# A two-layer AdaLN feed-forward kernel on one core: half-wide turns in the opening, two bias rows sent through DRAM, the last down chunk and one query product moved

## The chip, the cores and the metric

The kernel runs on one NeuronCore of a Trainium2 chip. Five engines work side by side, each with its own instruction queue: TensorE (matrix products and turns, PE in the profile), VectorE (DVE), ScalarE (ACT), GpSimd (POOL) and the queue of SyncE (SP), which here only issues DMAs. They meet through semaphores. The metric is the device time of one execution in microseconds; lower is better.

## The reference

The input x is 32 samples of 32 channels by 512. Two layers are added to it one after the other:

```python
# layer 0: grouped conv (9 taps), plus a row per sample and channel
h = conv1d(x, w, groups=4, pad=4) + (cond @ c_weight.T)[:, :, None] + bias
shared = relu(h @ up_w) ** 2 @ down_w
routed = ((h @ fc1) @ expert) * sum_of_top2(h @ gate_w) @ fc2
x = x + layernorm(shared + routed) * gamma + beta
# layer 1: per-sample mixing of channels, att from a small MLP on cond
att = softmax(gelu(gelu(cond @ W0 + b0) @ W1 + b1) @ W2 + b2)
y = einsum(att @ weight, x) + (att @ bias_k)[:, :, None]
q, k = y @ Wq.T, y @ Wk.T                  # 8 experts of 32
s = softmax(sum(q * k) per expert / sqrt(32))
x = x + y @ W.T + b + sum_e s_e * (y @ A_e.T) @ B_e.T
```

All is float32. Large products are made of three products of rounded halves: with a = a_hi + a_lo, a @ b is a_hi b_hi + a_hi b_lo + a_lo b_hi (`mm3`, lines 1215 to 1219).

## The kernel before, in words

The 1024 rows (sample, channel) are 8 tiles of 128, `T` from 0 to 7, in two halves `h` of four tiles. The order of work on each engine is written out by hand, and an engine does its list strictly in that order.

**Opening (lines 1410 to 1449).** TensorE multiplies ones seven times while the first loads land, turns the padded conv weights in 12 transposes of 128x128 (line 1418) and the conditioning rows in one (line 1424), and does the convs of tiles 0 to 3 (`conv`, line 1233). ScalarE and VectorE make the shifted copies of x that the convs read. VectorE forms the 32 context rows (`rows`, line 991: conditioning product plus bias) and folds them by a 0/1 mask into `fold128`, 32 samples wide, of which TensorE's products with ones spread the rows over the partitions: `conv_bias` (line 1246) adds samples 0 to 15 to the conv banks of the first half, and one product at line 1448 makes `B0`, the rows of samples 16 to 31 on all partitions, which ScalarE copies out (line 722). `B0` is used by `add_ctx` (line 873) in the second half. Between them the expert weight is multiplied with fc2 (12 products, lines 1441 to 1446).

**Each half (lines 1495 to 1521).** There are 8 chunks of the hidden dimension. `up(i)` makes chunk i in PSUM bank `U[i % 2]`; ScalarE takes `relu` of it (line 666), VectorE squares it (909), ScalarE rounds it into `R_hi` (672), VectorE writes the rest into `R_lo` (913, semaphore `s_R`). `up(i)` for i of 2 or more waits for `s_R` of chunk i-2, since it takes its bank. `down(i)` adds chunk i into the four banks `D[t]`. The first two chunks are made in parts of 256 columns: `up(0)` and `up(1)` left, `up(0)` right, `gate_rows` (lines 1257, 1258), `up(1)` right, `gate_logits`, `up(2)`, two `latent` products, and then `down` and `up` in turn. ScalarE does relu of chunk 0, `gate_copy`, `up_split` of chunk 0, relu of chunk 1. In the first half VectorE splits the four tiles of `H` (line 884) and up weights (863) in the order H0, up0, H1, up1, H2, H3. The buffer `relu` lies in the memory that the opening's small buffers, `rows` among them, had.

**Between the halves.** At the end of the first half TensorE does `down(6)`, `mixing` (lines 1461, 1466), `down(7)`, `conv(4)`, `mixing_bias` (line 1476: two products with ones that spread the 32 rows att @ bias_k, folded by VectorE with the mask, over the partitions; ScalarE copies them to `B1`), `conv(5)` to `conv(7)`, and the second half's `up(8)`. VectorE does per tile `norm_stats` (three instructions, lines 947 to 956), then, once GpSimd has the reciprocal root, `norm_apply` (line 964, semaphore `s_x1`), and `add_ctx` and `split_H` (873, 889) for tiles 4 to 7. The four parts of `down(8)` wait for `s_x1` of tiles 0 to 3, `up(8)` for the split tiles.

**Tail (lines 1524 to 1553).** Per tile `mix`, `qk` (24 products of 320 columns), `dense` (12 of 512), `turn_hw` and `combine`; `qk(7)` waits for the split weights of tile 5 (`s_hwT`, line 1154), whose bank it takes. `finish` adds into X, and SP stores it.

**The queues of DMA.** SP issues all weight loads at the start in one row: x in four parts, up, fc, down (2 MB), the last 1 MB of x, gamma, beta (`rowb`), then waits for the fc2 split, and issues the conditioning loads, three of the mixing weights and 32 of Wq and Wk. ScalarE issues only the store of the gate sums (`sum_rows`), its spread, and the last output.

Of the kernel before, what the change touches and what calls it, by code (L numbers as in the profile page):

```python
# [16 lines left out]
def bass_adaln_ffn(  # L17
# [84 lines left out]

    sum_rows = nc.dram_tensor("sum_rows", [HALVES, P, TPH], F32, kind="Internal").ap()

    with ExitStack() as ctx:
# [65 lines left out]
        aggb_hl = sb("aggb_hl", [2 * N, C], F32R)  # L171
        attT3 = sb("attT3", [96, N], F32R)
        attT2 = sb("attT2", [KE, 2, N])
        turn2 = sb("turn2", [2 * N, N])
        bk = sb("bk", [KE, C])
        with ExitStack() as early:
            def se(name, shape):
                return sb(name, shape, F32, early)
            cc_nat = se("cc_nat", [P, CD])
# [5 lines left out]
            wc_pad = se("wc_pad", [P, NWIN * PH + PH - 1, C])  # L185
            gmask = se("gmask", [C, G])
            exraw = se("exraw", [P, LC, LAT])
# [37 lines left out]
        fold2 = H_lo[0:2 * N, 0:2].rearrange("k a b -> k (a b)").rearrange("k (n o) -> k n o", o=C)  # L225
        agg = qk_raw[0:C].rearrange("i c a q -> i (c a q)")[:, 0:N * C].rearrange("i (o n) -> i o n", n=N)
        fold128 = up_hi[:, IC - 2:IC].rearrange("k c p q -> k (c p q)").rearrange("k (n o) -> k n o", o=C)
# [31 lines left out]
        s_ccz = sem("s_ccz")  # L259
# [13 lines left out]
        s_rowsb = sem("s_rowsb")  # L273
# [3 lines left out]
        s_B0p = sem("s_B0p")  # L277
# [22 lines left out]
        s_B1p = sem("s_B1p")  # L300
# [153 lines left out]
        def _(sp):  # L454
# [22 lines left out]
            sp.dma_start(rowb[:], L0_ffn_ln_beta.partition_broadcast(P)).then_inc(ld_gb, 16)  # L477
            sp.wait_ge(s_fc2, 1)
# [4 lines left out]
            sp.dma_start(b2, L1_cond_b2.partition_broadcast(N)).then_inc(ld_cond, 16)  # L483
            sp.wait_ge(s_wkz, 1)
# [138 lines left out]
        def _(act):  # L623
# [87 lines left out]
            split_up(1)  # L711
            split_H(2)
            split_H(3)
            act.wait_ge(ld_gate, 16)
# [6 lines left out]
            act.wait_ge(s_B0p, 1)  # L721
            nc.scalar.activation(B0[:], M[1], ACT.Copy).then_inc(s_B0, 1)
# [20 lines left out]
            def copy_attT():  # L743
                act.wait_ge(s_aTp, 1)
                nc.scalar.activation(attT3[:], M[0][0:96, 0:N], ACT.Copy).then_inc(s_aT, 1)
                nc.scalar.activation(attT2[:], bcast_mid(M[0][0:KE, 0:N], 2), ACT.Copy).then_inc(s_aT, 1)

            def make_B1():
                for i in range(2):
                    act.wait_ge(s_B1p, i + 1)  # L750
                    nc.scalar.activation(B1[:, i * BANK:(i + 1) * BANK], M[i], ACT.Copy).then_inc(s_B1, 1)

            for h in range(HALVES):
                i0 = h * IC
                if h:
                    make_B1()
# [94 lines left out]
        def _(dve):  # L851
# [14 lines left out]
            def add_ctx(T):  # L866

                dve.wait_ge(s_conv, T + 1)
                if T == TPH:
                    dve.wait_ge(s_B0, 1)  # L870
# [97 lines left out]
            nc.vector.memset(cc_nat[N + C:P], 0.0).then_inc(s_ccz, 1)  # L968
# [15 lines left out]
            def fold_rows(to, hl):  # L984

                return nc.vector.tensor_tensor(to, bcast_mid(hl[:].bitcast(F32), N),
                                               turn2[:].unsqueeze(2).broadcast_to([2 * N, N, C]), ALU.mult)

# [10 lines left out]
            fold_rows(fold, rows_hl).then_inc(s_rows, 1)  # L999
# [6 lines left out]
            split_up(1)  # L1006
            split_H(2)
            split_H(3)
            dve.wait_ge(s_gateh, 1)
# [37 lines left out]
            def fold_aggb():  # L1047
                dve.wait_ge(s_aggbp, 1)
                nc.vector.tensor_copy(aggb_hl[:], U[0][0:2 * N, 0:C]).then_inc(s_aggb, 1)
                dve.wait_ge(s_aggb, 1)  # L1050
                nc.vector.tensor_tensor(aggb_hl[N:2 * N], U[0][N:2 * N, 0:C], aggb_hl[N:2 * N].bitcast(F32),
                                        ALU.subtract).then_inc(s_aggb, 1)
                dve.wait_ge(s_aggb, 2)
                fold_rows(fold2, aggb_hl).then_inc(s_rowsb, 1)
# [8 lines left out]
            for h in range(HALVES):  # L1063
                i0 = h * IC
                if h:
                    split_attT()
                    fold_aggb()
                    turn_agg()
                    norm_stats(0)
                    norm_stats(1)  # L1070
                    norm_apply(0)
                    norm_stats(2)
                    norm_apply(1)
                    add_ctx(TPH)
                    norm_apply(2)
                    split_H(TPH)
                    for T in range(TPH + 1, TILES):
                        add_ctx(T)
                        split_H(T)
                    norm_stats(3)  # L1080
                    norm_apply(3)
                up_square(i0)
                up_split(i0)
                gate_sum(h)
                up_square(i0 + 1)
                if h == 0:
                    split_E2()
                up_split(i0 + 1)
                if h == 0:
# [24 lines left out]
            def y_bias(T):  # L1114

                dve.wait_ge(s_yp, T + 1)
                b = mix_bank(T)
# [96 lines left out]
        def _(pe):  # L1214
# [6 lines left out]
            def conv(T):  # L1221

                if T == TPH:
                    pe.wait_ge(s_R, IC)
                    pe.wait_ge(s_aggb, 2)
                if T == TPH + 2:
                    pe.wait_ge(s_lat, LC)
                    pe.wait_ge(s_B1, 2)
# [32 lines left out]
            def gate_logits(h):  # L1261

                pe.wait_ge(s_gTs, h + 1)
                if h == 0:
                    pe.wait_ge(s_B0, 1)
                else:
# [6 lines left out]
            def up(i, part=None):  # L1273
# [4 lines left out]
                if part is None:  # L1278
                    part = slice(0, TOKH)
                if c < 2:  # L1280
                    pe.wait_ge(s_H, TPH * h + part.stop // P)
# [4 lines left out]
                for p in range(PH):  # L1286
                    last = mm3(U[i % 2][:, part], up_hi[:, c, p], up_lo[:, c, p], H_hi[:, p, part],
                               H_lo[:, p, part], p == 0, p == PH - 1)
                if part.stop == TOKH:
                    last.then_inc(s_upp, 1)  # L1290
# [73 lines left out]
            def dense(T):  # L1364
# [4 lines left out]
                for p in range(PH):  # L1369
# [53 lines left out]
            pe.wait_ge(s_ccz, 1)  # L1423
            nc.tensor.transpose(M[0][:, 0:P], cc_nat[:], ident[:]).then_inc(s_cTp, 1)
# [16 lines left out]
            for lc in range(LC):  # L1441
                for mc in range(LC):
# [13 lines left out]
            def mixing():  # L1456
# [4 lines left out]
                nc.tensor.matmul(U[0][0:2 * N, 0:C], attT2[:].rearrange("k a n -> k (a n)"), bk[:],  # L1461
# [7 lines left out]

            def mixing_bias():  # L1470

                pe.wait_ge(s_rowsb, 1)
                pe.wait_ge(s_agg, 2)
                flat = fold2.rearrange("k n o -> k (n o)")
                for i in range(2):
                    nc.tensor.matmul(M[i], ones_r[0:2 * N, :], flat[:, i * BANK:(i + 1) * BANK],  # L1476
                                     start=True, stop=True).then_inc(s_B1p, 1)
# [105 lines left out]
```

## Time and profile before

| | us |
|---|---|
| median of 3 runs (219.13 to 219.44) | 219.26 |
| the profiled execution | 220.35 |
| its span, first to last instruction | 218.4 |
| TensorE busy | 214.3 (98%) |
| VectorE busy | 126.8 (58%) |
| ScalarE busy | 81.1 (37%) |
| GpSimd busy | 62.0 (28%) |

```profile
## 2 busy tenths in 40 slices
PE   7999999999999999999999999999999999999995
PEld 7999988888887778998888888888998998999984
DVE  4895455869725579876462034445996537435443
ACT  6694853549484621224322033442013112121110
POOL 3037221340464622119400002443354202202000
PEclk9999999999999999999999999999999999999999
DMA  6999944400000000046534000000000110110103
```

A slice is 5.46 us, and each digit is the busy share of an engine in tenths. TensorE shows 9 throughout. The sixteen DMA engines are full up to the fifth slice, that is to about 27 us, and half busy for three slices more. A busy TensorE is not TensorE at its peak, since matmuls are pipelined; the chain of work that ended last says how much time each group takes.

### The profile page before, as it was taken

How to read it: one execution, taken by the hardware profiler on the slowest of the kernel's cores; microseconds unless marked ns; L12 is line 12 of the kernel's file. 1: busy time of each engine (PE TensorE's matmuls, PEld its weight loads, DVE VectorE, ACT ScalarE, POOL GpSimd, SP SyncE). 2: the span in 40 equal slices, each digit the busy share in tenths (PEclk: the TensorE clock that was granted, in tenths of full speed). 3: DMA queues.
4: the chain of work that ended last, by engine and by line, in shares of the span. 5: the costliest groups of instructions: out<-in, count | busy, mean ns of one | idle time of the engine just before them, and what ended most of it. 6: DMA issues, size and time to landing. Idle time of an engine off the chain costs nothing.

```text
span 218.4 us, 3221 instructions
## 1 busy us (share of the span) xinstructions
PE 214.3 (98%) x1210; PEld 188.6 (86%) x1210; DVE 126.8 (58%) x268; ACT 81.1 (37%) x157; POOL 62.0 (28%) x77
## 2 busy tenths in 40 slices
PE   7999999999999999999999999999999999999995
PEld 7999988888887778998888888888998998999984
DVE  4895455869725579876462034445996537435443
ACT  6694853549484621224322033442013112121110
POOL 3037221340464622119400002443354202202000
PEclk9999999999999999999999999999999999999999
DMA  6999944400000000046534000000000110110103
GB/s 150 328 411 405 271 68 98 63 0 0 3 0 0 0 0 3 0 65 102 104 42 79 3 0 0 0 0 5 0 0 0 48 51 0 50 51 0 48 0 144
DMA packets 31087, 14.14 MB, mean 65 GB/s; under 512 B 25224, under 2 KB 26056, under 8 KB 31072
## 3 DMA queue, kind: packets, MB, share of 16 engines
q1 hardware_dynamic: 30256, 13.26, 22.2%
q10 hardware_dynamic: 816, 0.69, 1.1%
q8 instruction: 9, 0.15, 0.3%
q14 instruction: 6, 0.05, 0.1%
HBM read 11.84 MB, written 2.10 MB: 64 GB/s over the span
## 4 chain that ended last, share of the span: by engine, by line
PE 97%; DVE 1%; issue 0%; ACT 0%; DVEq 0%
PE PS L1217 26%; PE PS L1219 25%; PE PS L1218 25%; PE PS L1233 10%; PE PS L1346 3%; PE PS L1408 2%; PE PS L1418 1%; PE PS L1258 1%; PE PS L1257 1%; PE PS L1246 0%; PE PS L1375 0%; DVE ring L913 0%; PE PS L1476 0%; PE PS L1466 0%; ACT ring L672 0%
## 5 line engine op out<-in xcount | busy, mean ns | idle before, releaser
L909 DVE TENSOR_TENSOR PS<-PS,relu 128x512 f32<-128x512 f32 x16 | 11.2, 699 | 31.9 <-ACT relu L666 31.7
L1217 PE MATMUL PS<-H_hi,up_hi 128*128 128x512 f32 (+1 forms) x80 | 28.3, 354 | 0.2 <-DVE ring L913 0.2
L1219 PE MATMUL PS<-H_hi,up_lo 128*128 128x512 f32 (+1 forms) x80 | 27.8, 347 | 0.0
L1218 PE MATMUL PS<-H_lo,up_hi 128*128 128x512 f32 (+1 forms) x80 | 27.8, 347 | 0.0
L1233 PE MATMUL PS<-wconv,XS 128*128 128x128 f32 x192 | 22.5, 276 | 0.0
L1233 PEld LDWEIGHTS PS<-wconv,XS 128*128 128x128 f32 x192 | 21.9, 192 | 0.6 <-issue 0.4
L1217 PE MATMUL PS<-qkT_hi,H_hi 128*128 128x320 f32 x64 | 19.8, 310 | 0.1
L1219 PE MATMUL PS<-qkT_hi,H_lo 128*128 128x320 f32 x64 | 19.8, 309 | 0.0
L1218 PE MATMUL PS<-qkT_lo,H_hi 128*128 128x320 f32 x64 | 19.8, 309 | 0.0
L588 POOL TENSOR_TENSOR X<-X,rowb 128x512 f32<-128x512 f32 x8 | 10.3, 1297 | 28.1 <-PE PS L1346 28.1
L1217 PE MATMUL PS<-dn_hi,ring 128*128 128x512 f32 x44 | 17.4, 395 | 0.0
L666 ACT ACTIVATE relu<-PS 128x512 f32<-128x512 f32 x16 | 9.5, 593 | 21.2 <-PE PS L1219 19.5
L1219 PE MATMUL PS<-dn_hi,ring 128*128 128x512 f32 x44 | 17.2, 390 | 0.0
L1218 PE MATMUL PS<-dn_lo,ring 128*128 128x512 f32 x44 | 17.1, 389 | 0.0
L1217 PEld LDWEIGHTS PS<-H_hi,up_hi 128*128 128x128 f32 x80 | 15.1, 189 | 2.2 <-issue 0.3
L1219 PEld LDWEIGHTS PS<-H_hi,up_lo 128*128 128x128 f32 x80 | 15.1, 189 | 1.9
L1218 PEld LDWEIGHTS PS<-H_lo,up_hi 128*128 128x128 f32 x80 | 15.2, 189 | 1.9
L560 POOL TENSOR_TENSOR dn_lo<-dn_raw,dn_hi 128x512 fp32r<-128x512 f32 x8 | 10.3, 1290 | 21.7 <-ACT dn_hi L648 21.7
L450 ACT ACTIVATE XS<-X 32x128 f32<-32x128 f32 (+2 forms) x24 | 15.8, 658 | 0.6 <-DMA X<-in_x_dram 0.3
L449 DVE COPY XS<-X 32x128 f32<-32x128 f32 (+2 forms) x40 | 15.2, 380 | 0.6
L592 POOL TENSOR_TENSOR wT_lo<-qk_raw,wT_hi 128x512 fp32r<-128x512 f32 x4 | 5.1, 1291 | 31.9 <-ACT wT_hi L700 31.9
L1217 PE MATMUL PS<-wT_hi,H_hi 128*128 128x512 f32 (+1 forms) x36 | 13.7, 381 | 0.0
(196 smaller groups left out, 477.3 us busy)
## 6 DMA issues: line engine op xcount, KB each, us to landing
up_raw<-in_L_ffn_up_w_dram SPq DMA_DIRECT2D x2, 1024.0 KB, 9.7
dn_raw<-in_L_ffn_down_w_dram SPq DMA_DIRECT2D x2, 1024.0 KB, 13.9
out_dram<-X SPq DMA_DIRECT2D x7, 256.0 KB, 2.0
X<-in_x_dram SPq DMA_DIRECT2D x1, 1024.0 KB, 15.1
XS<-in_L_ffn_W_dram SPq DMA_DIRECT2D x16, 64.0 KB, 2.4
X<-in_x_dram SPq DMA_DIRECT2D x2, 256.0 KB, 3.4
X<-in_x_dram SPq DMA_DIRECT2D x1, 512.0 KB, 5.8
fc<-in_L_ffn_fc_w_dram SPq DMA_DIRECT2D x1, 512.0 KB, 6.4
```

Of the source, the lines that this page charges most:

```text
L449: return nc.vector.tensor_copy(dst, src)
L450: return nc.scalar.activation(dst, src, ACT.Copy)
L560: nc.gpsimd.tensor_tensor(dn_lo[:, c, :], dn_raw[:, c, :], dn_hi[:, c, :].bitcast(F32), ALU.subtract).then_inc(s_dn, 1)
L588: nc.gpsimd.tensor_tensor(X[:, T, :], X[:, T, :], rowb[:], ALU.add).then_inc(s_x1b, 1)
L592: nc.gpsimd.tensor_tensor(wg_dst(g, False), wg_turned(g), wg_dst(g, True).bitcast(F32), ALU.subtract)\
L666: nc.scalar.activation(relu[:], U[i % 2], ACT.Relu).then_inc(s_relu, 1)
L909: nc.vector.tensor_tensor(U[i % 2], U[i % 2], relu[:], ALU.mult).then_inc(s_sq, 1)
L1217: nc.tensor.matmul(o, lh, rh, start=start, stop=False)
L1218: nc.tensor.matmul(o, lh, rl, start=False, stop=False)
L1219: return nc.tensor.matmul(o, ll, rh, start=False, stop=stop)
L1233: last = nc.tensor.matmul(conv_bank(T)[:, s * P:(s + 1) * P], XS[:, T % TPH * SPT + s, a:a + P], wconv[:, a], start=(a == 0 and (T >= TPH ...
L1346: last = nc.tensor.matmul(mix_bank(T)[:, p, :], X[:, T, p * P:(p + 1) * P], BD[:, T], start=True, stop=True)
```

## The change

1. The padded conv weights and the conditioning rows get 64 partitions for 128, and the 13 transposes take a 64x64 identity: 64 columns for 128. The memset on the unused rows goes.
2. The context rows are folded for 16 samples only. `B0` is made by DMA: SP stores 16 rows to DRAM and reads them back spread over the partitions; the product of line 1448 and its copy go. Relu of chunk 0 now also waits for the store, whose source it overwrites.
3. `B1` goes the same way, late: the fold, `mixing_bias` and its copies go.
4. `up(0)`, `up(1)`, `up(8)` and `up(9)` are made in whole columns; the splits of H2 and H3 go ahead of the one of up1.
5. `down(7)` comes after the convs of the second half, and VectorE's norm steps between the ones of the second half.
6. In the tail a quarter of `dense(6)` comes between `combine(4)` and `qk(7)`.

```diff
@@ sync
+            sp.wait_ge(s_ctx, 1)
+            sp.dma_start(ctx_rows, rows[N // 2:N]).then_inc(s_ctxw, 16)
             sp.wait_ge(s_fc2, 1)
...
             sp.dma_start(b2, L1_cond_b2.partition_broadcast(N)).then_inc(ld_cond, 16)
+            sp.wait_ge(s_ctxw, 16)
+            sp.dma_start(B0[:], ctx_rows.rearrange("n o -> (n o)").partition_broadcast(P)).then_inc(s_B0, 16)
             sp.wait_ge(s_wkz, 1)
...
+            sp.wait_ge(s_aggb, 1)
+            sp.dma_start(mix_rows, aggb[:]).then_inc(s_mixw, 16)
+            sp.wait_ge(s_mixw, 16)
+            sp.dma_start(B1[:], mix_rows.rearrange("n o -> (n o)").partition_broadcast(P)).then_inc(s_B1, 16)
             sp.wait_ge(s_xb, TILES)
@@ scalar
             def up_relu(i):
                 act.wait_ge(s_upp, i + 1)
+                if i == 0:
+                    act.wait_ge(s_ctxw, 16)
...
-            split_up(1)
             split_H(2)
             split_H(3)
+            split_up(1)
...
-            act.wait_ge(s_B0p, 1)
-            nc.scalar.activation(B0[:], M[1], ACT.Copy).then_inc(s_B0, 1)
@@ vector
-            fold_rows(fold, rows_hl).then_inc(s_rows, 1)
+            nc.vector.tensor_tensor(fold, bcast_mid(rows_hl[:].bitcast(F32), N // 2),
+                                    turn2[:, 0:N // 2].unsqueeze(2).broadcast_to([2 * N, N // 2, C]), ALU.mult)\
+                .then_inc(s_rows, 1)
...
-            def fold_aggb():
+            def copy_aggb():
                 dve.wait_ge(s_aggbp, 1)
...
+                nc.vector.tensor_copy(aggb[:], U[1][0:N, 0:C]).then_inc(s_aggb, 1)
...
                 if h:
                     split_attT()
-                    fold_aggb()
+                    copy_aggb()
                     turn_agg()
+                    for T in range(TPH, TILES):
+                        add_ctx(T)
+                        split_H(T)
                     norm_stats(0)
                     norm_stats(1)
                     norm_apply(0)
+                up_square(i0)
+                if h:
                     norm_stats(2)
+                up_split(i0)
+                if h:
                     norm_apply(1)
...
+                else:
+                    gate_sum(h)
+                up_square(i0 + 1)
+                if h:
+                    gate_sum(h)
                     norm_stats(3)
...
                 up_split(i0 + 1)
+                if h:
+                    norm_apply(2)
+                    norm_apply(3)
@@ tensor
-                    last = nc.tensor.transpose(M[1][:, o0:o0 + P],
-                                               wc_pad[:, k0:k0 + PH, :].rearrange("p k c -> p (k c)"), ident[:])
+                    last = nc.tensor.transpose(M[1][:, o0:o0 + 2 * C],
+                                               wc_pad[:, k0:k0 + PH, :].rearrange("p k c -> p (k c)"),
+                                               ident[0:2 * C, 0:2 * C])
...
-            nc.tensor.matmul(M[1], ones_r[:], fold128[:, N // 2:N, :].rearrange("k n o -> k (n o)"),
-                             start=True, stop=True).then_inc(s_B0p, 1)
...
                 if h:
                     conv(TPH)
-                    mixing_bias()
                     for t in range(1, TPH):
                         conv(TPH + t)
-
-                for i in (h * IC, h * IC + 1):
-                    up(i, slice(0, TOKH // 2))
-                up(h * IC, slice(TOKH // 2, TOKH))
+                    down(IC - 1)
+
+                up(h * IC)
                 gate_rows(h)
-                up(h * IC + 1, slice(TOKH // 2, TOKH))
+                up(h * IC + 1)
                 gate_logits(h)
                 up(h * IC + 2)
                 for n in range(LC):
                     latent(h * LC + n)
-                for c in range(IC):
+                for c in range(IC if h else IC - 1):
                     down(h * IC + c)
...
             combine(a)
+            dense(c, range(0, 1))
             qk(d)
-            dense(c)
+            dense(c, range(1, PH))
```

## Rows read from the trace of the kernel before

**Rows 1.** part 4 of the page: the chain that ended last, by engine
```profile
PE 97%; DVE 1%; issue 0%; ACT 0%; DVEq 0%
```

**Rows 2.** waits of TensorE: tile, line <- releaser: us in total, times, longest
```profile
PE PS L1217 <- DVE ring L913: 0.2, 1, 0.2
```

**Rows 3.** chain that ended last, 4 to 32 us: start us, us, what
```profile
4.47 2.56 PE PS L1418 x12
...
13.46 0.44 PE PS L1401 x4
...
22.97 0.23 PE PS L1448
...
31.32 0.47 PE PS L1217
```

**Rows 4.** timeline of TensorE, 23 to 28 us: start, us, line, operation, shapes, count
```profile
23.15 0.28 PE L1218 MATMUL PS<-H_lo,up_hi 128*128 128x256 f32 x1
...
27.23 0.28 PE L1219 MATMUL PS<-H_hi,up_lo 128*128 128x256 f32 x1
```

**Rows 5.** timeline of VectorE, 14 to 39 us
```profile
14.54 0.18 DVE L991 TENSOR_TENSOR rows<-PS,fsb 64x32 f32<-64x32 f32 x1
...
22.56 1.28 DVE L884 TENSOR_TENSOR H_lo<-PS,H_hi 128x512 fp32r<-128x512 f32 x2
...
30.49 0.69 DVE L913 TENSOR_TENSOR ring<-PS,ring 128x512 fp32r<-128x512 f32 x1 [1.60 <-ACT ring L672]
...
38.45 0.69 DVE L913 TENSOR_TENSOR ring_last<-PS,ring_last 128x512 fp32r<-128x512 f32 x1 [0.66 <-ACT ring_last L672]
```

**Rows 6.** timeline of ScalarE at 36 us
```profile
36.47 0.58 ACT L666 ACTIVATE relu<-PS 128x512 f32<-128x512 f32 x1
```

**Rows 7.** timeline of the SP queue, 16 to 42 us
```profile
16.17 1.25 SPq L477 DMA_DIRECT2D rowb<-in_L_ffn_ln_beta_dram  x1
...
32.54 8.81 SPq L494 DMA_DIRECT2D qk_raw<-in_L_ffn_Wk_dram  x16
```

**Rows 8.** DMA issues: count, KB each, median us from issue to landing
```profile
out_dram<-X SPq DMA_DIRECT2D x7, 256.0 KB, 2.0
...
rowb<-in_L_ffn_ln_beta_dram SPq DMA_DIRECT2D x1, 256.0 KB, 11.4
...
sum_rows<-ssum ACTq DMA_DIRECT2D x2, 2.0 KB, 3.0
```

**Rows 9.** chain that ended last at 85 us
```profile
85.44 0.65 PE PS L1476 x2
```

**Rows 10.** timeline of TensorE, 102 to 111 us
```profile
102.52 0.40 PE L1218 MATMUL PS<-H_lo,up_hi 128*128 128x512 f32 x1
...
104.81 0.39 PE L1219 MATMUL PS<-H_hi,up_lo 128*128 128x512 f32 x1
...
110.48 0.39 PE L1217 MATMUL PS<-dn_hi,ring_last 128*128 128x512 f32 x1
```

**Rows 11.** timeline of VectorE, 59 to 97 us
```profile
59.33 0.70 DVE L943 STREAM_TRANSPOSE fc_raw<-qk_raw 128x512 f32<-128x512 f32 x1
...
84.08 0.69 DVE L947 BATCH_NORM_STATS2 st<-PS 128x6 f32<-128x512 f32 x1
...
85.69 0.74 DVE L964 SCALAR_TENSOR_TENSOR X<-PS,rstd,X 128x512 f32<-128x512 f32 x1
...
94.58 0.68 DVE L873 TENSOR_TENSOR tf<-PS,B 128x512 f32<-128x512 f32 x1
95.97 0.69 DVE L889 TENSOR_TENSOR H_lo<-tf,H_hi 128x512 fp32r<-128x512 f32 x1 [0.70 <-ACT H_hi L660]
```

**Rows 12.** chain that ended last, 203 to 205 us
```profile
203.89 0.08 issue
203.97 0.39 PE PS L1217
204.36 0.15 PE PS L1218
```

More of the change, by code:

```diff
@@ L101, in bass_adaln_ffn @@
     out_dram = out.rearrange("(t s) c l -> (s c) t l", s=SPT)
+    ctx_rows = nc.dram_tensor("ctx_rows", [N // 2, C], F32, kind="Internal").ap()
+    mix_rows = nc.dram_tensor("mix_rows", [N, C], F32, kind="Internal").ap()
     sum_rows = nc.dram_tensor("sum_rows", [HALVES, P, TPH], F32, kind="Internal").ap()
@@ L170, in bass_adaln_ffn @@
         cT = sb("cT", [CD, 4, N])
-        aggb_hl = sb("aggb_hl", [2 * N, C], F32R)
+        aggb = sb("aggb", [N, C])
         attT3 = sb("attT3", [96, N], F32R)
-        attT2 = sb("attT2", [KE, 2, N])
+        attT2 = sb("attT2", [KE, 2 * N])[:, 0:N]
         turn2 = sb("turn2", [2 * N, N])
@@ L224, in bass_adaln_ffn @@
         wk3 = lat_hi[0:96].rearrange("k a b -> k (a b)").rearrange("k (o i) -> k o i", o=C)
-        fold2 = H_lo[0:2 * N, 0:2].rearrange("k a b -> k (a b)").rearrange("k (n o) -> k n o", o=C)
         agg = qk_raw[0:C].rearrange("i c a q -> i (c a q)")[:, 0:N * C].rearrange("i (o n) -> i o n", n=N)
-        fold128 = up_hi[:, IC - 2:IC].rearrange("k c p q -> k (c p q)").rearrange("k (n o) -> k n o", o=C)
+        fold128 = up_hi[:, IC - 2:IC].rearrange("k c p q -> k (c p q)").rearrange("k (n o) -> k n o", o=C)[:, 0:N // 2]
         fold = fold128[0:2 * N]
@@ L276, in bass_adaln_ffn @@
         s_wconv = sem("s_wconv")
-        s_B0p = sem("s_B0p")
+        s_ctxw = sem("s_ctxw")
         s_B0 = sem("s_B0")
@@ L299, in bass_adaln_ffn @@
         s_BD = sem("s_BD")
-        s_B1p = sem("s_B1p")
+        s_mixw = sem("s_mixw")
         s_B1 = sem("s_B1")
@@ L745, in copy_attT @@
                 nc.scalar.activation(attT3[:], M[0][0:96, 0:N], ACT.Copy).then_inc(s_aT, 1)
[L746 to L751, printed above, removed]
+                nc.scalar.activation(attT2[:], M[0][0:KE, 0:N], ACT.Copy).then_inc(s_aT, 1)
             for h in range(HALVES):
@@ L869, in add_ctx @@
                 if T == TPH:
-                    dve.wait_ge(s_B0, 1)
+                    dve.wait_ge(s_B0, 16)
                 if T >= TPH + 2:
@@ L1071, in _ @@
                     norm_apply(0)
+                up_square(i0)
+                if h:
                     norm_stats(2)
+                up_split(i0)
+                if h:
                     norm_apply(1)
[L1074 to L1079, printed above, removed]
-                    norm_stats(3)
[L1081 to L1085, printed above, removed]
+                else:
[3 more added lines that the diff above has]
+                    gate_sum(h)
+                    norm_stats(3)
                 if h == 0:
@@ L1116, in y_bias @@
                 dve.wait_ge(s_yp, T + 1)
+                if T == 0:
+                    dve.wait_ge(s_B1, 16)
                 b = mix_bank(T)
@@ L1224, in conv @@
                     pe.wait_ge(s_R, IC)
-                    pe.wait_ge(s_aggb, 2)
+                if T == TPH + 1:
+                    pe.wait_ge(s_aggb, 1)
                 if T == TPH + 2:
                     pe.wait_ge(s_lat, LC)
-                    pe.wait_ge(s_B1, 2)
+                    pe.wait_ge(s_agg, 2)
                 for s in range(SPT):
@@ L1271, in gate_logits, with up @@
                 last.then_inc(s_gp, 1)
-            def up(i, part=None):
+            def up(i):
                 h, c = divmod(i, IC)
@@ L1277, in up @@
                     pe.wait_ge(s_up, c + 1)
-                if part is None:
-                    part = slice(0, TOKH)
                 if c < 2:
-                    pe.wait_ge(s_H, TPH * h + part.stop // P)
+                    pe.wait_ge(s_H, TPH * (h + 1))
                     if h:
@@ L1286, in up @@
                 for p in range(PH):
[L1287 to L1290, printed above, removed]
+                    last = mm3(U[i % 2], up_hi[:, c, p], up_lo[:, c, p], H_hi[:, p], H_lo[:, p],
+                               p == 0, p == PH - 1)
+                last.then_inc(s_upp, 1)
             def latent(n):
@@ L1362, in qk, with dense @@
                 last.then_inc(s_qkp, 1)
-            def dense(T):
+            def dense(T, parts=range(PH)):
                 ts = slice(T % TPH * P, (T % TPH + 1) * P)
@@ L1368, in dense @@
                     pe.wait_ge(s_x1, TPH + T + 1)
-                for p in range(PH):
+                for p in parts:
                     mm3(D[T % TPH], H_hi[:, p, ts], H_lo[:, p, ts], wT_hi[:, p], wT_lo[:, p], p == 0, False)
@@ L1468, in mixing @@
                 last.then_inc(s_AGp, 1)
[L1470 to L1477, printed above, removed]
             def conditioning(c):
```

28 lines of the change are left out of this document (6 added, 22 removed).

## The prediction

> **What bounds the kernel now.** I read the chain of waits first: TensorE holds 97% of it [rows 1]. Then TensorE's own waits: apart from the start there is one, of 0.2 us, for the R_lo split of chunk 0 ahead of `up(2)` [rows 2]. So TensorE's list is the bound nearly everywhere. Work off TensorE (masks, copies, norm steps) is worth nothing until it makes TensorE wait, a shortened product is worth its full length, and a new wait costs what TensorE lacks in other work. Last I read the timelines around the places that the diff touches, and the landing of the DMAs, because the diff puts a store between the opening and the first relu.
>
> **The half-wide turns.** The 12 transposes take 2.56 us, 213 ns each, while four later ones of the same 128x128 take 0.44 us, 110 ns each [rows 3]: here TensorE still runs at the lower of its two levels (1.2 GHz against 2.4). With 64 columns instead of 128 one can't cost less than half, 107 ns, nor more than now, so the gain is 0 to 1.3 us. No row shows a 64-column turn in this stage. The load of 128 weight columns stays and a copy of the weights must still pass ScalarE, so I take 0.8. The late engines, not the turns, then set the next steps: the H splits that `up(0)` waits for end at 22.56 + 1.28 = 23.84 in the trace [rows 5]. With the up1 split (0.65) behind them and 0.8 earlier, they end at 22.4.
>
> **Whole columns.** From the second to the 36th product of 256 columns 34 steps take 27.23 - 23.15 = 4.08 us, 120 ns each [rows 4]; ten of 512 take 2.29, 229 ns each [rows 10]. Per half 48 of the first (5.76) give way to 24 of the second (5.50): 0.26 us. The price is that `up(0)` and `up(8)` wait for all four tiles, which is in the starts worked out here.
>
> **B0 out of TensorE's list** saves 0.23 us [rows 3]. So without a further wait TensorE would come to `up(2)` at 31.32 - 0.20 (its wait) - 0.23 - 0.26 - 0.8 = 29.8, or by the H splits 22.4 + 0.1 + 24 products of 229 ns (5.5) + eight gate products of the same width (1.8) and the four small gate turns (0.35, an estimate by the 110 ns of a turn, a little less each) = 30.2. I take 30.2 against 31.32 [rows 3].
>
> **The store that relu of chunk 0 waits for.** This is what decides the opening. SP can issue it only after `rowb`, whose issue ends at 16.17 + 1.25 = 17.42 [rows 7]; its data are ready well before (14.54) [rows 5]. But `rowb`, issued at 16.17, lands 11.4 us later, at 27.57, since the weight loads and the last inputs stand ahead of it [rows 7, 8]. The store stands behind `rowb` in the same queue. Its 16 rows of 128 bytes are no load; its place is. Landing L: at least 27.6 if it ends together with `rowb`; at most 27.6 + 3.0 = 30.6 if the whole time of the small store `sum_rows` from issue to landing comes on top, or + 2.0 by the output stores [rows 8]. Issue and start lie under the backlog, so only the end of that time should remain; I take 0.8, L = 28.4, which is nearer to the lower end.
>
> What hangs on L: relu is first in ScalarE's list, behind it stand `gate_copy` and R_hi of chunk 0, and VectorE's square and R_lo wait for these. In chunk 2, from the start of relu to the end of R_lo, this took 38.45 + 0.69 - 36.47 = 2.67 us [rows 5, 6]; the gate copy fits into the time in which VectorE squares. Then 0.14 until TensorE goes on (R_lo 30.49 + 0.69 = 31.18, product at 31.32) [rows 3, 5], and 0.1 from landing to relu. So `up(2)` starts at L + 2.9 = 31.3, TensorE's own work being done at 30.2. It stands for 1.1 us, and against 31.32 nothing is won: the transposes, the missing product, the whole columns of the first half and the order of the splits are hidden by the store. Opening: 0, with 0.8 gained at L = 27.6 and 2.2 lost at 30.6.
>
> The Trainium skill, DMA: Bandwidth & Descriptors, section "Queues, rings and completion order", says that one issuing engine has one ring on each DMA engine, consumed in ring order; by that the store can't pass `rowb`. The same page (section "Anatomy of one DMA") puts a fixed 2 us on a transfer, mostly the receipt of the target memory, longest for HBM. By it L would be 29.6 and the opening lose 1.2 us. The rows above allow this, and it is a rival below.
>
> SP also waits for this store before it issues B0's load, the mixing weights and Wq and Wk. The last of these 32 issues ends at 32.54 + 8.81 = 41.35 [rows 7]; it moves to about L + 20 = 48.4, and lands some 2 us later, against the first use of Wq at 59.33 [rows 11]: 9 us of cover, if the landings keep to that. B0 itself is needed in the second half.
>
> **Between the halves.** `mixing_bias` goes: 0.65 us of TensorE [rows 9]. Its two copies and the mask product were beside other work. `down(7)` is only moved. It is now what hides the last splits: from the start of `add_ctx(7)` to the end of its H_lo, 95.97 + 0.69 - 94.58 = 2.08 us [rows 11], against 12 products of 229 ns, 2.75. So `up(8)` finds its tiles with some 0.5 us to spare, and starts 0.65 earlier than now. Whole columns save another 0.26.
>
> What is late next is VectorE. Its norm steps begin only after the split of tile 7, which comes 2.75 + 0.65 = 3.4 us earlier than now (96.66), at 93.3. Until `down(8)` (110.48 - 0.9 = 109.6 [rows 10]) it must do four stats of 1.61 us (85.69 - 84.08), four applies of 0.74 [rows 11], two chunks' square and R_lo (2.8) and the gate sum (about 0.8): 13.0 us in 16.3. The waits for relu and the gate eat part of the rest; I put the fourth `s_x1` at 107, over 2 us early. So nothing is lost, and the bound from the other side is 1 us, should these waits add up. B1's store, load and the shifted bias load are issued after 118 us with nothing behind them until about 146: 0.
>
> **Tail.** Ahead of `qk(7)` the chain shows 0.08 of issue and a first product of 0.39, where the next takes 0.15 [rows 12]: 0.32 us of waiting for the split of tile 5. A quarter of `dense(6)` (three products, 0.69) covers it, and delays the scores of tile 7, whose turn comes five us later. Gain 0.3, bounds 0 and 0.35.
>
> **Sum.** 0 + 0.65 + 0.26 + 0.3 = 1.2 us. The profiled execution took 220.35 (span 218.4 and 1.95 around it); it becomes 219.15. The median of the runs is 1.09 below the profiled time, so it goes from 219.26 to 218.05. I forecast 218.0.
>
> **The rivals.**
>
> *A, the store lands a little later (15%).* L = 29.6, by the whole 2.0 us of a quiet store [rows 8] after `rowb`. `up(2)` starts at 32.5, the opening loses 1.2, all that the rest gains: 219.3, no change. For it: the target is DRAM; against it: most of those 2.0 us are paid under the backlog.
>
> *B, slower: the first relu as the bottleneck (13%, with 6% for smaller causes of the same sign).* L = 30.6 or later, `up(2)` at 33.5: minus 2.2 in the opening, plus 1.2 elsewhere, 220.3. From L = 29.6 on the change is a loss, one us for each us. TensorE would then stand for over 3 us, and might fall to its lower level, which would cost some more. For it: the sixteen DMA engines are full until 27 us, and the store needs the slowest of them. Against it: no small DMA that queued behind something is seen to pay its full time anew.
>
> *C, the store is no gate (12%).* It lands before 27.2, as it would if the engines took it between the loads. `up(2)` starts at 30.2: 1.1 gained in the opening, 2.3 in all, 216.9.
>
> *D, the norm steps gate `down(8)` (7%).* The move of `down(7)` turns TensorE's 0.9 us between the halves into a wait: 219.0. It decides once VectorE's chain is over 2 us longer than worked out. The slack speaks against it, the strict order of a list with four waits for relu and gate in it for it.
>
> **How the numbers follow.** The forecast holds 47%, with a range of its own from 217.4 (L = 27.8) to 218.7 (L = 29.1). A, B, C and D are given above. The range 216.8 to 220.4 takes in C, A and D whole and B in part. A difference of 0.2%, 0.44 us, is about what a measurement of this kernel can tell from none. Faster than that: the forecast, C and half of D, less a rest of the forecast near 218.8, 0.61. Same: A and the rest of D, with that part, 0.2. Slower: B and what goes with it, 0.19.
>
> **What would show it.** `up(2)` in TensorE's timeline at 31.3, after a pause of about 1 us, and relu of chunk 0 starting near 28.5 with the store named as its releaser; an earlier relu shows C, one near 29.7 A, one past 30.7 B. The first 12 transposes in 1.3 to 2.1 us. The stretch from `conv(4)` to the end of `up(9)` shorter by 0.65 + 0.26, with no wait ahead of `up(8)` or `down(8)`. No first product of 0.39 in `qk(7)`. The prediction is wrong if the store's landing isn't tied to the end of the loads, or if TensorE shows a pause over 0.3 us anywhere after `up(2)`.

## The result and the profile after

The changed kernel took 217.63 us, the median of 8 executions, against 219.39 of the kernel before in the same comparison: ratio 0.9922, 95% interval 0.9901 to 0.9943. It is faster, inside the range and 0.4 us below the forecast. The profiled execution took 217.47, span 215.7.

One thing must be known for every number below. The executions of the changed kernel fall into two groups with nothing between: six at 217.47 to 217.66 and two at 219.09 and 219.64. Twelve more (e1) gave four at 217.53 to 217.74 and eight at 219.2 to 219.54, so that median was 219.27. The kernel before has no such gap: the 29 executions beside e1 lie from 219.17 to 220.41, no two neighbours more than 0.21 apart. The page prints full clock over the whole span for both groups (the same row of nines), so the cause has to be read from durations. The profile after is one of the lower group.

The page of the kernel after, part 4, and under it TensorE's waits (line <- releaser: us, times, longest):

```profile
PE 92%; DVE 4%; DMA 1%; issue 0%; ACT 0%; DVEq 0%
```

```profile
PE PS L1215 <- DVE H_lo L885: 0.4, 1, 0.4
```

Against [rows 1, 2]: TensorE still holds nearly all of the chain, but VectorE's share rose from 1% to 4%. The wait for R_lo ahead of `up(2)` is gone, one of 0.4 for the last H split ahead of `up(0)` has come. Apart from the start there is no other.

The timeline of TensorE, kernel after, at the places that the prediction named (start us, us, line, operation, shapes, count, idle before):

```profile
4.40 0.96 PE L1412 MATMUL PS<-ident,wc_pad 64*128 64x64 f32 x12
5.20 0.22 PE L1418 MATMUL PS<-ident,cc_nat 64*128 64x64 f32 x1
5.35 0.66 PE L1402 MATMUL PS<-ones 128*128 128x128 f32 x4
6.12 2.92 PE L1232 MATMUL PS<-wconv,XS 128*128 128x128 f32 x24
...
22.29 0.47 PE L1215 MATMUL PS<-H_hi,up_hi 128*128 128x512 f32 x1 [0.44 <-DVE H_lo L885]
...
30.10 0.50 PE L1215 MATMUL PS<-H_hi,up_hi 128*128 128x512 f32 x1
...
78.08 0.66 PE L1457 MATMUL PS<-lat_hi,attT 96*32 96x512 f32 x2
...
92.06 0.39 PE L1215 MATMUL PS<-H_hi,up_hi 128*128 128x512 f32 x1
...
108.09 0.39 PE L1215 MATMUL PS<-dn_hi,ring_last 128*128 128x512 f32 x1
```

From the first turn to the next instruction it is 5.20 - 4.40 = 0.80 us, 67 ns each, where [rows 3] had 2.56 for the twelve. `up(2)` starts at 30.10 against 31.32 [rows 3], without a wait; `down(8)` at 108.09 against 110.48 [rows 10].

The store and what hangs on it, kernel after, first SP's queue, then the DMA issues (KB each, us from issue to landing), then ScalarE and VectorE:

```profile
15.81 0.52 SPq L476 DMA_DIRECT2D rowb<-in_L_ffn_ln_beta_dram  x1
16.38 0.59 SPq L478 DMA_DIRECT2D ctx_rows<-rows  x1
```

```profile
rowb<-in_L_ffn_ln_beta_dram SPq DMA_DIRECT2D x1, 256.0 KB, 10.4
...
ctx_rows<-rows SPq DMA_DIRECT2D x1, 2.0 KB, 10.0
```

```profile
26.49 0.60 ACT L675 ACTIVATE relu<-PS 128x512 f32<-128x512 f32 x1 [1.37 <-DMA ctx_rows<-rows]
```

```profile
28.48 0.69 DVE L914 TENSOR_TENSOR ring<-PS,ring 128x512 fp32r<-128x512 f32 x1 [0.67 <-ACT ring L681]
...
90.88 0.69 DVE L890 TENSOR_TENSOR H_lo<-tf,H_hi 128x512 fp32r<-128x512 f32 x1 [0.70 <-ACT H_hi L667]
...
103.70 1.40 DVE L965 SCALAR_TENSOR_TENSOR X<-PS,rstd,X 128x512 f32<-128x512 f32 x2
```

`rowb` lands at 15.81 + 10.4 = 26.21, against 27.57 [rows 7, 8], and the store at 16.38 + 10.0 = 26.38, 0.17 us behind it. relu does wait for the store, but R_lo ends at 28.48 + 0.69 = 29.17, 0.9 before `up(2)`: a wait of ScalarE that TensorE never sees. From the start of relu to the end of R_lo it is 2.68 us, as worked out (2.67).

The chain that ended last, kernel after, in the opening and in the tail:

```profile
9.28 2.94 PE PS L1232 x24
...
202.18 0.14 PE PS L1215
```

Up to 9.28 us the chain runs over VectorE's shifted copies of X, seventeen of some 0.27 us from 4.03 on, and not over TensorE. In the tail the first product of `qk(7)` costs what its neighbours do (0.15); the 0.39 and the issue of 0.08 of [rows 12] are gone.

### The profile page after: what moved, and what is told of

The parts are those of the page before. It is cut to its first block, busy times and chain, and to the rows that moved or that the text cites. A ratio compares the mean times of both kernels' runs of the same rounds, so it can differ in the third digit from the quotient of the medians.

```text
span 215.7 us, 3111 instructions
## 1 busy us (share of the span) xinstructions
PE 211.2 (98%) x1159; PEld 183.5 (85%) x1159; DVE 123.5 (57%) x265; ACT 79.7 (37%) x154; POOL 61.7 (29%) x77
## 4 chain that ended last, share of the span: by engine, by line
PE 92%; DVE 4%; DMA 1%; issue 0%; ACT 0%; DVEq 0%
PE PS L1215 26%; PE PS L1217 25%; PE PS L1216 25%; PE PS L1232 9%; PE PS L1340 3%; DVE XS L448 2%; DVE H_lo L885 1%; DMA wc_nat<-in_L_cond_weight_dram 1%; PE PS L1257 1%; PE PS L1256 1%; PE PS L1369 0%; PE PS L1266 0%; DVE wc_pad L973 0%; ACT H_hi L662 0%; DVE up_lo L864 0%
## 5 line engine op out<-in xcount | busy, mean ns | idle before, releaser
L1215 PE MATMUL PS<-H_hi,up_hi 128*128 128x512 f32 x64 | 25.6, 400 | 0.4 <-DVE H_lo L885 0.4
L1217 PE MATMUL PS<-H_hi,up_lo 128*128 128x512 f32 x64 | 25.0, 390 | 0.0
L1216 PE MATMUL PS<-H_lo,up_hi 128*128 128x512 f32 x64 | 25.0, 390 | 0.0
L1215 PEld LDWEIGHTS PS<-H_hi,up_hi 128*128 128x128 f32 x64 | 12.0, 188 | 3.2 <-issue 0.8
L1217 PEld LDWEIGHTS PS<-H_hi,up_lo 128*128 128x128 f32 x64 | 12.0, 188 | 2.6
L1216 PEld LDWEIGHTS PS<-H_lo,up_hi 128*128 128x128 f32 x64 | 12.0, 188 | 2.4
L1217 PE MATMUL PS<-wT_hi,H_lo 128*128 128x512 f32 (+1 forms) x36 | 13.2, 367 | 0.0
```

Of the source, the lines that this page charges most:

```text
L1215: nc.tensor.matmul(o, lh, rh, start=start, stop=False)
L1216: nc.tensor.matmul(o, lh, rl, start=False, stop=False)
L1217: return nc.tensor.matmul(o, ll, rh, start=False, stop=stop)
```

## The experiments

Theory after the first comparison: the gain is the missing product, the whole columns and the tail; the store is no gate; and the halved turns make the two groups, since the work ahead of the first conv no longer brings TensorE to its upper level (2.4 GHz) in every execution. Rival: the groups come from the order of the split and the store, or lie in the chip and would show with any kernel.

**e1, e2: both kernels again.** No edit.

> The changed kernel as it is, for its spread and one more trace. Theory (level): each kernel has two groups of times by the moment at which TensorE rises to its upper level in the opening; the changed kernel lands near 217.6 in most executions and 1 to 2 us higher in some, and a trace of the first group shows the 12 narrow turns at under 80 ns each. Rival (the change made the rise early): all traces of it rise early and the higher times have another cause, in which case its slower executions say nothing on the opening. Both expect a median of 217.6.

> The kernel before as it is. Theory (level): median 219.3, and a trace in which the 12 turns take about 110 ns each instead of 213, with up(2) at about 30.4 us instead of 31.3; the trace read for the prediction was one of the late rise and 1 us long. Rival (wide turns keep the level low): the turns take 213 ns again and up(2) starts at 31.3, and the difference of 1 us between profile and median has another place.

Measured: e1 as told above, ratio 0.9961 (0.9937 to 0.9984); e2 219.14 to 220.35, median 219.48. The trace of e1 is one of its upper group (219.28), the trace of e2 is the shortest of its executions (219.14). TensorE in e1, then in e2:

```profile
4.39 1.54 PE L1412 MATMUL PS<-ident,wc_pad 64*128 64x64 f32 x12
5.73 0.31 PE L1418 MATMUL PS<-ident,cc_nat 64*128 64x64 f32 x1
5.97 1.11 PE L1402 MATMUL PS<-ones 128*128 128x128 f32 x4
6.88 4.37 PE L1232 MATMUL PS<-wconv,XS 128*128 128x128 f32 x24
...
11.23 2.92 PE L1232 MATMUL PS<-wconv,XS 128*128 128x128 f32 x24
...
31.90 0.50 PE L1215 MATMUL PS<-H_hi,up_hi 128*128 128x512 f32 x1
```

```profile
4.22 1.47 PE L1418 MATMUL PS<-ident,wc_pad 128*128 128x128 f32 x12
5.53 0.27 PE L1424 MATMUL PS<-ident,cc_nat 128*128 128x128 f32 x1
...
30.29 0.47 PE L1217 MATMUL PS<-H_hi,up_hi 128*128 128x512 f32 x1 [0.20 <-DVE ring L913]
...
78.29 0.66 PE L1466 MATMUL PS<-lat_hi,attT 96*32 96x512 f32 x2
...
109.45 0.39 PE L1217 MATMUL PS<-dn_hi,ring_last 128*128 128x512 f32 x1
```

Read the same line in both executions of the changed kernel. In the upper group the turns take (5.73 - 4.39) / 12 = 112 ns instead of 67, the four ones products 1.11 instead of 0.66 and the first 24 conv products 4.37 instead of 2.92: TensorE is at its lower level (1.2 GHz) until about 10 us and comes to the upper one inside `conv(0)`. The record of the granted clock in the packed trace says the same by where it begins, full from there on: at 9.96 us in e1, at 4.41 in the trace of the lower group, 7.08 in the profile behind [rows 3] and 4.17 in e2. Where it has no entry the page prints full clock. From there on nothing differs, and `up(2)` is 1.80 late, which is the distance of the groups (219.28 - 217.47 = 1.81). The Trainium skill, TensorE: Matmul & The Clock Gate, Part 1 ("The HAM clock gate"), says that the number of products run at the lower level varies from execution to execution of one kernel, and puts the penalty at under 1% of a typical kernel's span. The traces agree: 1.8 of 219 us is 0.8%.

And the kernel before has this too, only smaller: its turns took 213 ns each in the profile that I predicted from [rows 3] and (5.53 - 4.22) / 12 = 109 in e2, with `up(2)` at 31.32 and 30.29. I had worked from one of the longer executions.

**e3: the turns 128 columns wide again.**

```
-            wc_pad = se("wc_pad", [2 * C, ...])
+            wc_pad = se("wc_pad", [P, ...])
-   transpose(M[1][:, o0:o0 + 2 * C], ..., ident[0:2 * C, 0:2 * C])
+   transpose(M[1][:, o0:o0 + P], ..., ident[:])
```

The turn of the conditioning rows and its memset go back with them.

> The changed kernel with the 13 turns at 128 columns again. Theory (hidden turns): the shifted copies on VectorE set the first convs once TensorE is at its upper level, so 12 turns at 110 ns for 67 (0.5 us) are hidden for the most part: 217.6 to 217.9. Rival (turns on the path): the whole 0.5 us shows, 218.1, or 1.8 us, 219.4, if the wide turns also keep TensorE at its lower level.

Measured: 217.87 to 218.63 in six executions, median 218.41, ratio 0.9938 (0.992 to 0.9956). No group at 219.4. TensorE in e3:

```profile
4.26 2.43 PE L1414 MATMUL PS<-ident,wc_pad 128*128 128x128 f32 x12
6.52 0.27 PE L1421 MATMUL PS<-ident,cc_nat 128*128 128x128 f32 x1
...
7.26 2.94 PE L1234 MATMUL PS<-wconv,XS 128*128 128x128 f32 x24
```

The first twelve take 2.26 us here, most of them at the lower level, yet the conv behind them runs at the upper one. Here the rise comes at 6.2 us (the clock record begins at 6.19), inside the turns; in e1 it came after them.

**e4: `up` of the first two chunks in column halves again.**

```
-                up(h * IC)
-                gate_rows(h)
-                up(h * IC + 1)
+                for i in (h * IC, h * IC + 1):
+                    up(i, slice(0, TOKH // 2))
+                up(h * IC, slice(TOKH // 2, TOKH))
+                gate_rows(h)
+                up(h * IC + 1, slice(TOKH // 2, TOKH))
```

The order of the splits goes back with it.

> The changed kernel with up in parts of 256 columns in both halves, in the order of before, and the split of up1 ahead of H2 and H3. Theory: both halves pay 24 more products, 0.26 us each by their durations, and the first half gets back the wait for all four tiles (0.4): 217.6 + 0.26 + 0.26 - 0.4 = 217.7 to 217.9. Rival (whole columns are worth more than their durations, by the weight loads that come with each product): 218.2 or more.

Measured: seven executions at 217.59 to 217.88 and five at 219.36 to 219.76, ratio 0.9941 (0.9915 to 0.9966). The two groups stay, each 0.15 to 0.3 above those of e1. Its trace is of the upper group, as is that of e1. TensorE in e4:

```profile
11.49 2.92 PE L1232 MATMUL PS<-wconv,XS 128*128 128x128 f32 x24
...
32.04 0.47 PE L1215 MATMUL PS<-H_hi,up_hi 128*128 128x512 f32 x1 [0.20 <-DVE ring L914]
...
79.99 0.66 PE L1458 MATMUL PS<-lat_hi,attT 96*32 96x512 f32 x2
...
110.39 0.39 PE L1215 MATMUL PS<-dn_hi,ring_last 128*128 128x512 f32 x1
```

`up(2)` is 0.14 later than in e1, but in this execution the rise came later too, and `conv(1)`, the second 24 conv products, starts 0.26 later (11.49 against 11.23). From `conv(1)` to `up(2)` it is 20.55 us here and 20.67 in e1 (20.65 and 20.64 in e10 and e12, where TensorE's list up to there is that of e1). So in the opening whole columns lose 0.1: the 0.44 of waiting is more than they save. Between the halves, from the mixing product to `down(8)`, it is 30.40 against 30.01: they give 0.39 there. Together that is the 0.15 to 0.3 of the groups. The order of the splits has nothing to do with the groups.

**e5, e6, e7: what makes the two groups.** e5 puts two more ones products behind the narrow turns, e6 takes the kernel before and narrows its turns alone, e7 has wide turns and one ones product less ahead of them.

```
e5  -            warm(1)
    +            warm(3)
e6  (kernel before)
    -   transpose(M[1][:, o0:o0 + P], ..., ident[:])
    +   transpose(M[1][:, o0:o0 + 2 * C], ..., ident[0:2 * C, 0:2 * C])
e7  (kernel after, wide turns as in e3)
    -            warm(7)
    +            warm(6)
```

> The changed kernel with three products of ones instead of one behind the narrow turns (0.45 us more at the upper level). Theory (the narrow turns make TensorE idle enough to rise late): the fuller stretch ahead of the convs brings back the rise at 6 to 7 us, so the group at 219.3 to 219.5 goes, and times lie from 217.6 to 218.6. Rival (what stands behind the turns doesn't matter, it is the turns themselves): two groups stay, 217.7 and 219.6.

> The kernel before with the 13 turns at 64 columns and nothing else changed. Theory: times split in two groups, one at 218.9 to 219.2 with the early rise and one at 221 with a rise near 10 us, where before spreads from 219.15 to 220.4. Rival (the two groups of the changed kernel come from another part, the store or the whole columns): one group, at 219.0, no execution over 220.5.

> The changed kernel with 128-column turns and six products of ones instead of seven ahead of them, so that the turns begin 0.4 us earlier in the opening (the padded weights are there at 3.84 us). Theory: no group at 219.4; in executions with a rise at 6 to 7 us the convs start up to 0.4 us earlier than with seven, so times from 217.7 to 218.4, median 218.1. Rival (less work before the turns makes the rise late): a group above 219.

Measured: e5 six at 217.48 to 217.84 and six at 219.43 to 219.96, ratio 0.9958 (0.9927 to 0.999). e6 ten at 219.14 to 219.63 and two at 220.98 and 221.29, ratio 0.9997 (0.9975 to 1.0018). e7 217.68 to 218.36 in six, median 217.97, ratio 0.992 (0.9901 to 0.9939). TensorE in e6 (e7 has 2.18 us in that place, 128 columns wide, from 4.08):

```profile
4.40 1.01 PE L1416 MATMUL PS<-ident,wc_pad 64*128 64x64 f32 x12
```

e6 settles whose doing the groups are: the narrow turns by themselves open a group at 221.0 to 221.3, above each of the 28 executions of the kernel before beside it (219.16 to 220.39), and their lowest time, 219.14, is that kernel's own (e2). So they gain nothing where TensorE rises early, since `conv(0)` and `conv(1)` are then fed by VectorE's copies. What they change is when it rises. With wide turns the clock records begin at 4.2 (e2), 4.4 (e8), 5.5 (e7), 6.2 (e3) and 7.1 us (the profile behind [rows 3]); with narrow ones at 4.2 to 5.3 (the kernel after, e5, e9, e11) or only at 10.0 to 10.6 (e1, e4, e10, e12). The times show both sides of it: ten executions of e6 end by 219.63, above which 13 of the 28 lie, and two pay for that; the means are 219.62 and 219.65. My idea that more work behind the turns would bring the rise in time fell with e5. What exactly TensorE needs there I have not found. e7 is the best version by the mean, 217.96 in its six executions against 218.48 in the changed kernel's 20: above the lower group by 0.3 us, but without the upper one, in which 10 of those 20 fell.

**e8: the kernel before with B1 alone through DRAM.**

```
-                    mixing_bias()
-                    make_B1()
+            sp.dma_start(mix_rows, aggb[:]).then_inc(s_mixw, 16)
+            sp.wait_ge(s_mixw, 16)
+            sp.dma_start(B1[:], mix_rows...partition_broadcast(P)).then_inc(s_B1, 16)
```

> The kernel before with the mixing bias alone sent through DRAM: no fold, no two products, no copies. Theory: TensorE's list loses 0.65 us at 85 us and nothing else changes, so every execution is 0.65 us shorter, from 218.5 to 219.8, median 218.8. Rival (what is taken out there is filled by a wait for the norm steps or the splits): 219.3, no change.

Measured: 218.12 to 219.3, median 218.78 against 219.6, ratio 0.996 (0.9946 to 0.9975). TensorE in e8:

```profile
78.19 0.66 PE L1463 MATMUL PS<-lat_hi,attT 96*32 96x512 f32 x2
...
108.50 0.39 PE L1213 MATMUL PS<-dn_hi,ring_last 128*128 128x512 f32 x1
```

From the mixing product to `down(8)`: 109.45 - 78.29 = 31.16 in e2, 108.50 - 78.19 = 30.31 in e8. The two products cost 0.85, not the 0.65 of [rows 9], and the medians say the same (0.82). The other 0.2 is in no row of its own; it goes within the stretch of the 96 convs (11.56 us in the chain of e2, two products included, 10.72 in that of e8), so I put it down to convs being broken off for a product of another shape. No run inserts such a product alone.

**e9, e10: the store.** e9 keeps the rows in memory of their own, so that relu need not wait for the store; e10 issues the store only behind the conditioning and mixing weights.

```
e9  -            rows = se("rows", [2 * N, C])
    +        rows = sb("rows", [2 * N, C])          (behind bk)
    -                if i == 0:
    -                    act.wait_ge(s_ctxw, 16)
e10 the three lines that store ctx_rows, wait for it and load B0
    stand behind the load of L1_cond_weight
```

> The changed kernel with the context rows in memory of their own, so that the first relu doesn't wait for their store. Theory (the store has slack): relu of chunk 0 starts about 1 us earlier and nothing after it moves, since TensorE comes to up(2) after R_lo of chunk 0 in either case: the two groups at 217.6 and 219.4 as in the changed kernel. Rival (the store is the gate, as predicted): up(2) starts 0.5 us or more earlier and the times fall by as much.

> The changed kernel with the store of the context rows issued behind the conditioning and mixing loads, at about 23.5 us instead of 16.4. Theory (a small store ends with what stands ahead of it, plus 0.2 us): it lands near 28 us, up(2) starts 2.9 us after that, at about 31, with VectorE's R_lo as releaser: 0.8 us late, 218.4 in the lower group. Rival 1 (the small loads ahead are nothing): lands before 27.2, no change. Rival 2 (a store that isn't under the backlog pays 2 to 3 us anew): lands at 29 or later, up(2) at 32, 219.4 in the lower group.

Measured: e9 five at 219.06 to 219.37 and five at 220.7 to 221.16, ratio 1.0015 (0.999 to 1.0041). e10 217.53 to 219.55, six of the ten at 218.1 to 218.98, median 218.81, ratio 0.9953 (0.9934 to 0.9973). ScalarE and TensorE in e9, then SP's queue and the DMA issue of e10:

```profile
25.36 0.60 ACT L673 ACTIVATE relu<-PS 128x512 f32<-128x512 f32 x1 [0.18 <-PE PS L1215]
```

```profile
30.13 0.50 PE L1213 MATMUL PS<-H_hi,up_hi 128*128 128x512 f32 x1
```

```profile
22.22 0.32 SPq L488 DMA_DIRECT2D ctx_rows<-rows  x1
```

```profile
ctx_rows<-rows SPq DMA_DIRECT2D x1, 2.0 KB, 5.2
```

e9 answers its question: relu starts 1.13 us earlier and `up(2)` does not move (30.13 against 30.10). The store is no gate of TensorE, though the margin is thin. In e9 the store landed at 27.43, later than in any other trace in which it follows `rowb` at once; by 2.9 us from there it would, with the wait in place, have held `up(2)` until 30.3, an estimate, against 30.13. That the kernel got 1.6 us slower nonetheless was not expected. No wait came. The products themselves are longer; the groups of TensorE's products from 110 to 140 us (count, busy us, mean ns), in the kernel after and in e9:

```profile
L1216 PE MATMUL PS<-dn_lo,ring 128*128 128x512 f32 x12 | 4.7, 389 | 0.0
```

```profile
L1214 PE MATMUL PS<-dn_lo,ring 128*128 128x512 f32 x12 | 4.7, 395 | 0.0
```

About 5 ns each for those whose operands lie in the ring and the latent buffers, none in the convs (the distance is 0.03 us at `up(2)`, 0.6 at 76 us and at `down(8)`, 1.7 at the end). The rows moved these buffers up by 128 bytes. But in the same stretch products of H_hi with the up weights are longer too, and those lie ahead of the rows and did not move (389 ns in the kernel after, in e9 393):

```profile
L1213 PE MATMUL PS<-H_hi,up_hi 128*128 128x512 f32 x18 | 7.1, 393 | 0.0
```

So the placement of a product's own operands does not seem to be the whole cause. Why e9 is 1.6 us slower stays open; no run moved the buffers alone.

e10 is largely inconclusive. Its store landed at 22.22 + 5.2 = 27.42, beyond the 27.2 from which it should hold up `up(2)`, but the trace is one with a late rise, where TensorE comes to `up(2)` only at 32.18 and sees nothing. The six times between 218.1 and 219, where no other kernel with narrow turns has any, would fit a delay of 0.5 to 1.4 us by the store in executions with an early rise. No trace shows it.

**e11: `down(7)` ahead of the convs again, with the norm steps where they were.**

```
                     for t in range(TPH):
                         conv(TPH + t)
-                    down(IC - 1)
-                for c in range(IC if h else IC - 1):
+                for c in range(IC):
```

> The changed kernel with down(7) back ahead of the convs and VectorE's norm steps back among the splits. Theory (down(7) is the cover of the last splits): up(8), in whole columns, waits for the split of tile 7, which ends some 2.1 to 2.4 us after the last conv: 217.6 + 2.2 = 219.8 in the lower group. Rival (the move is neutral, TensorE finds the tiles ready in either order): 217.6.

Measured: nine at 219.9 to 220.12 and three at 221.45 to 221.69, ratio 1.0033 (1.0012 to 1.0054). TensorE's waits in e11:

```profile
PE PS L1211 <- DVE H_lo L890: 2.2, 1, 2.2
```

The lower group is 2.4 us above that of the changed kernel (220.0 against 217.6), and 2.2 of it are this wait ahead of `up(8)`. The norm steps that went back with `down(7)` have no part in it: the last conv ends at 85.75 + 6.53 = 92.28, and VectorE takes up tile 7 at once, at 92.31, and ends its split 2.1 us later, at 93.70 + 0.69 = 94.39. `down(7)` in its new place is what covers it; without the move the rest of the change is a loss. Two of the three upper executions report a mean granted clock of 0.992, all others of this record 0.998 or more; which stage lost it no trace shows.

**e12: the query product of the tail back.**

```
-            dense(c, range(0, 1))
             qk(d)
-            dense(c, range(1, PH))
+            dense(c)
```

> The changed kernel with dense(6) whole behind qk(7). Theory: the first product of qk(7) waits for the split of tile 5 again, 0.32 us: 217.9 in the lower group, 219.7 in the upper. Rival (the wait was already absorbed by the turns of the last tiles): no difference.

Measured: seven at 217.73 to 218.08 and five at 219.31 to 219.74, ratio 0.995 (0.9926 to 0.9973): the lower group 0.15 to 0.25 up. The chain of e12 has the stall back, 0.09 of issue and then

```profile
203.52 0.38 PE PS L1215
```

## Why the prediction came out

The time was right; one step under it was wrong, and a second error hid that. The median had luck as well: six of the eight executions fell in the lower group. The same kernel again (e1) had four of twelve there and a median of 219.27, 1.3 above the forecast. The mean of all 20 is 218.48, that of the 29 executions of the kernel before beside e1 219.63: 1.15 gained, where I had added up 1.2. By steps:

- **The store: mis-sized.** I put its landing at `rowb` + 0.8 and `rowb` at 27.57. It was 0.17 after `rowb`, and the backlog itself ended 1.36 earlier (26.21), so L = 26.38 and not 28.4. The end of the backlog moves from execution to execution: `rowb` landed at 26.5 to 27.6 in the four traces of kernels without the store (27.57 was the last of them), at 26.0 to 27.2 in the nine in which the store follows it at once. As I had written, a landing before 27.2 makes the store no gate: this step is rival C, and `up(2)` started at 30.10 where C said 30.2. e9 shows it by taking the wait away. The ring order of the Trainium skill (DMA: Bandwidth & Descriptors, "Queues, rings and completion order") agrees with the traces, the store landed 0.1 to 0.3 us behind `rowb` in all nine; but the same section says that completion is not in the order of issue, so that the store "can't pass" was more than it gives. The fixed 2 us of "Anatomy of one DMA", a section on DMAs that GpSimd issues, did not come on top of the backlog here.
- **The execution I read was a long one.** C promised 216.9, since it took its gain in the opening from 31.32. In e2 `up(2)` stands at 30.29: the profile before held 1.0 us of late rise that the executions around the median hold in part or not at all. Between early-rise executions (e2 219.14, after 217.47) the opening gives only 0.2. The wrong landing and the missing gain cancelled, and that is luck: I said 0, it was 0.2.
- **The turns: bound too narrow, gain too large.** The bound of half, 107 ns, assumed the lower level. They took 67 ns at the upper and 112 at the lower one. Of the 0.8 I took, no execution with an early rise got anything (e6).
- **B0 out of the list and whole columns in the opening**: 0.49 of TensorE's work is gone, and the start of `up(0)` is later by the wait of 0.44 for all four tiles. By e4 whole columns lose 0.1 here, so the 0.2 of the opening is B0's product (0.23), an opening that began 0.1 earlier in the trace after (`conv(1)` at 9.28 against 9.38 in e2), and that loss.
- **Between the halves: 1.15** against 0.91 (31.16 - 30.01). `mixing_bias` gave 0.85 and not 0.65 (e8), whole columns 0.30 by the difference and 0.39 by e4, for 0.26.
- **`down(7)`**: the last split ends at 90.88 + 0.69 = 91.57, `up(8)` starts at 92.06: 0.5 of slack, as worked out; e11 shows the 2.2 that it covers. The fourth `s_x1` came at 103.70 + 1.40 = 105.1, 3 us before `down(8)`; rival D had nothing.
- **Tail**: 0.3 forecast, 0.3 left over of 1.67 after the other two, 0.15 to 0.25 by e12.
- **What no step foresaw**: the second group, 1.8 us up. My bounds of the turns had only their own durations in them, not what their shortness does to the level of what follows. It is not a rival that I gave, and by the share of executions in it (10 of 20) it costs the mean 0.9 us, as much as `mixing_bias` gives. A, B and D did not happen.

## What to carry to other kernels

Before a trace is used as the base of a sum, compare the durations of like products in its opening with those later on: the printed clock did not show a late rise, only the place where its record begins did. Work that TensorE does while it waits for something else anyway may still decide at which level the next stage runs, so shortening it can cost more than it gives. When a product goes, move what hid behind it in the same change.

## What the runs showed of the hardware

- With twelve turns of 64 columns ahead of the convs TensorE rose to its upper level at 4.2 to 5.3 us or only at 10.0 to 10.6 (eight traces); with 128 columns at 4.2, 4.4, 5.5, 6.2 and 7.1, and none of the 24 executions of e3, e7 and e8 lies in an upper group. Cost of the late rise: 1.8 us.
- A 64-column turn takes 67 ns at the upper level and 112 at the lower, a 128-column one 109 and 213.
- A store of 2 KB queued behind a full backlog landed 0.1 to 0.3 us after its predecessor (nine traces); alone, 2 KB took 3.0 [rows 8] and 2.0 in the kernel after.
- A buffer shift of 128 bytes (e9) went with products of 512 columns some 5 ns longer each, 389 to 395, but also with longer ones whose operands had not moved, 389 to 393 (not isolated, cause open).
- Two products of 512 columns on 64 rows between convs cost 0.85 us where their own time is 0.65 (e8).
